# Between the layers of a graph attention kernel: rows started during the last matmuls, one wait per quotient, normalising in place

## The chip, the core and the metric

One core of a Trainium2 chip runs the whole program. The metric is device time in microseconds (us), smaller is better. Two kernels are compared by the median of several runs.

## The reference

x has 4096 rows (nodes) of 256 features; `adj` is a 4096 x 4096 matrix of zeros and ones. Four layers follow one another, each as `x = layernorm(x + gnn(x, adj))`:

```
# layer 0: h = x W (4 heads of 64); e = leaky_relu(s_src + s_dst, 0.01), masked by adj
#          out = elu(softmax(e) @ h)
# layer 1: the same with slope 0.2 and without elu
# layer 2: one head of 256 with slope 0.2, and four dense side branches and a gate
# layer 3: h = tanh(x W + b); softmax over one score per node, masked by adj; att @ (x W)
x = _layernorm(x + _L0_gnn_ref(x, adj, ...), axis=-1)
x = _layernorm(x + _L1_gnn_ref(x, adj, ...), axis=-1)
```

The change is at the two joints from layer 0 to 1 and from 1 to 2.

## The kernel before

The rows are held as T = 32 tiles of 128 rows; four tiles are a quad (QT = 4, QUADS = 8). `x` and `h` (a view of `hv`) stay in SBUF for all tiles. Each engine has its own program, written out in order by hand, and waits on counting semaphores; there is no scheduler.

**Attention of layers 0 and 1.** There are four passes, one for each head, of eight groups of 512 rows (`group` in the PE and DVE programs). DVE makes 0/1 masks from the packed adjacency, ACT marks which scores are above the bend, and PE multiplies the masks with the bf16 parts of the values, in banks 0 to 3 or 4 to 7 in turn. `evacuate` (DVE) adds up four banks into `sums`; `quotient` (POOL) divides and writes the group's rows of `h`. Group g's quotient of the last pass completes the rows of quad g, since a group and a quad are the same 512 rows. The last group's banks are summed by an `evacuate` at the end of `attention`, when PE has finished; POOL then makes the last quotient. `values` has two slots, one for even and one for odd passes; the last pass reads slot 1.

**Joint.** DVE's loop over layers does, for layers 1 and 2: `fold_weights(l)` (eight small operations on the new weights), a wait for the last quotient of all, and `between(l)`. For a quad, `norm_stats` adds h to x (layer 1: after an ELU), and makes mean and variance; POOL's `make_rstd` makes the inverse root; `normalize` writes the four normalised tiles to a staging tile `xs`, which is shared by all quads. In the loop of `between`, DVE normalises quad q-1 and then starts `norm_stats` of quad q. The ELU of a quad is max(h, exp(min(h, 0)) - 1): ACT's `elu_exp` makes `low` and then `ex`, and DVE combines. ACT waits with `elu_exp(q)` until DVE has used `ex` of quad q-1, for there is one tile of each.

**Product.** For each quad, PE's `dense` transposes the eight blocks of `xs` into banks 0 and 1; ACT copies them to `xT` in two pieces; PE multiplies with the weights into banks 2 to 5 (sixteen matmuls), and ACT copies h and the scores of each tile out. From layer 1 on, ACT also copies `xs` back into `x`, and DVE waits for that (`s_xkept`) before the next `normalize`. In layer 0, POOL's `stage_x` copies x to `xs`, and PE packs the adjacency (`pack`) between the quads. All these are loops over q with registers (`Fori`).

The order in ACT's layer 1 is `elu_exp(0)`, then for q = 1 to 7 `elu_exp(q)` and `dense(1, q-1)`, then `dense(1, 7)`.

After the last quad come the scores' maximum, the exponentials and the first values, and then the next attention.

## Time and profile before

| what | value |
|---|---|
| median of 3 runs | 3223.1 us (3221.91 to 3226.79) |
| the profiled execution, its own time | 3223.3 us |
| its span, first to last instruction | 3221.5 us |
| PE busy (matmuls) | 2984.2 us, 93% |
| DVE, ACT, POOL busy | 69%, 60%, 38% |
| mean granted clock of PE | 0.973 |
| opening stage with layer 0's product | 24 to 81 us |
| joint of layers 0 and 1, last matmul to last copy of h | about 906 to 987 us |
| joint of layers 1 and 2, the same | about 1716 to 1777 us |

The page lists for each engine how long it was busy; a timeline lists single instructions with their start, their duration and, in brackets, how long the engine stood idle before them and what released it. VectorE is DVE, ScalarE is ACT, GpSimd is POOL in such rows. The granted clock is the share of full speed that TensorE had.

### The profile page before, as it was taken

To read this page: it belongs to the slowest core of one execution; us is meant where nothing else is said; L and a number is where in the kernel's file an instruction comes from. 1 tells how busy PE (TensorE), PEld (TensorE's weight loads), DVE (VectorE), ACT (ScalarE), POOL (GpSimd) and SP (SyncE) were. 2 spreads that over 40 slices of the span, in tenths; PEclk is the share of its full clock that TensorE was granted. 3 is DMA by queue.
4 is the path that set the end of the run, shared out by engine and by line. 5 is a ranking of instruction groups with operands and counts; after the bars stand their busy time and mean duration, and the time that the engine had idled before them with its cause. 6 is when DMAs were issued, how large, how long until landed. Compare 5 with 4: busy or idle time off the path is not lost.

```text
span 3221.5 us, 73270 instructions
## 1 busy us (share of the span) xinstructions
PE 2984.2 (93%) x26664; PEld 2737.6 (85%) x26664; DVE 2219.1 (69%) x4102; ACT 1932.2 (60%) x3404; POOL 1213.0 (38%) x1646
## 2 busy tenths in 40 slices
PE   6588899999966999999997899999999999879997
PEld 5588899999955999999996778778878878669997
DVE  4888688887767888788776555666666656554447
ACT  4565799999957999989995444444444544420000
POOL 2333454751212646565222013333333233534433
PEclk9899999999988999999999999999999999989999
DMA  7576000000100000000010000000000000000001
GB/s 267 185 251 217 11 10 13 14 10 14 67 0 11 13 14 10 13 12 12 14 42 0 14 4 4 1 4 4 1 4 4 1 1 1 2 1 1 0 0 52
DMA packets 42292, 104.64 MB, mean 32 GB/s; under 512 B 9904, under 2 KB 23472, under 8 KB 33968
## 3 DMA queue, kind: packets, MB, share of 16 engines
q1 hardware_dynamic: 42160, 102.92, 9.6%
q8 instruction: 78, 1.28, 0.2%
q14 instruction: 54, 0.44, 0.0%
HBM read 98.51 MB, written 4.39 MB: 32 GB/s over the span
## 4 chain that ended last, share of the span: by engine, by line
PE 85%; DVE 5%; issue 3%; DMA 2%; ACT 2%; POOL 1%; SPq 0%; DVEq 0%; POOLq 0%; ACTq 0%
PE bank L1104 21%; PE bank L1101 21%; PE bank L1147 15%; PE bank L1185 12%; PE bank L1107 11%; DMA arena<-in_adj_dram 2%; PE bank L1174 2%; PE bank L1065 2%; PE bank L1161 1%; PE bank L1079 1%; DVE arena L1414 1%; DVE sums L1624 1%; PE bank L1291 0%; DVE rings L1691 0%; POOL lnst L545 0%
## 5 line engine op out<-in xcount | busy, mean ns | idle before, releaser
L1101 PE MATMUL bank<-values,rings 128*128 128x195 bf16 x8192 | 1415.4, 247 | 91.6 <-DVE sums L1624 46.7
L832 ACT ACTIVATE above<-srow,kpass 128x512 fp8e4<-128x512 f32 x2048 | 1288.8, 709 | 213.2 <-DVE rings L1694 202.7
L1104 PE MATMUL bank<-values,rings 128*128 128x195 bf16 x8192 | 1415.3, 249 | 0.0
L1101 PEld LDWEIGHTS bank<-values,rings 128*128 128x128 fp8e4 x8192 | 809.4, 99 | 102.0 <-issue 98.4
L1104 PEld LDWEIGHTS bank<-values,rings 128*128 128x128 fp8e4 x8192 | 787.2, 96 | 1.2
L1691 DVE TENSOR_TENSOR rings<-rings,above 128x512 uint32<-128x512 uint32 x512 | 390.2, 762 | 240.5 <-PE bank L1104 208.9
L850 ACT ACTIVATE values<-srow,cmul 128x512 f32<-128x512 f32 x256 | 206.0, 815 | 432.8 <-PE bank L1185 431.8
L1694 DVE TENSOR_TENSOR rings<-rings 128x512 uint32<-128x512 uint32 x512 | 427.8, 836 | 17.5
L1185 PE MATMUL bank<-hv,values 128*128 128x257 f32 x1792 | 423.1, 381 | 10.0 <-DVE values L1568 10.0
L1185 PEld LDWEIGHTS bank<-hv,values 128*128 128x128 f32 x1792 | 336.4, 191 | 80.7 <-issue 25.5
L1107 PE MATMUL bank<-values,rings 128*128 128x195 bf16 x4096 | 348.0, 248 | 19.0 <-DVE rings L1682 19.0
L1107 PEld LDWEIGHTS bank<-values,rings 128*128 128x128 fp8e4 x4096 | 347.5, 97 | 19.7 <-issue 19.4
L577 POOL TENSOR_TENSOR quot<-sums,cmul 128x260 f32<-128x260 f32 x64 | 45.6, 712 | 714.2 <-DVE sums L1624 714.2
L1685 DVE TENSOR_SCALAR rings<-packed 128x512 uint32 (+1 forms) x512 | 245.5, 479 | 2.1 <-issue 1.4
L1682 DVE TENSOR_SCALAR rings<-packed 128x512 uint32 (+1 forms) x256 | 116.4, 455 | 175.1 <-PE bank L1107 173.2
L1568 DVE SCALAR_TENSOR_TENSOR values<-values,cmul,rings 128x512 f32<-128x512 f32 x256 | 192.9, 761 | 43.9 <-ACT values L850 43.5
L661 POOL TENSOR_SCALAR zrow<-zrow 128x1 f32<-128x1 f32 x128 | 47.6, 372 | 446.1 <-DVE zrow L1765 446.1
L1624 DVE TENSOR_REDUCE sums<-bank 128x130 f32<-128x390 f32 (+1 forms) x396 | 181.7, 487 | 14.9 <-PE bank L1104 13.2
L1147 PE MATMUL bank<-arena,above 128*128 128x256 f32 (+1 forms) x496 | 165.9, 482 | 0.8 <-ACT above L905 0.8
L1147 PEld LDWEIGHTS bank<-arena,above 128*128 128x128 f32 x496 | 94.0, 190 | 53.1 <-issue 43.9
L507 POOL TENSOR_TENSOR values<-vtmp_pool,values 128x260 f32 (+1 forms) x120 | 109.4, 912 | 25.5 <-POOL values L504 21.2
L1147 PE MATMUL bank<-quot,arena 128*128 128x256 f32 x512 | 118.3, 379 | 0.0
(202 smaller groups left out, 3500.5 us busy)
## 6 DMA issues: line engine op xcount, KB each, us to landing
arena<-in_adj_dram SPq DMA_DIRECT2D x64, 1024.0 KB, 5.5
srow<-src_dram SPq DMA_DIRECT2D x72, 256.0 KB, 3.2
x<-in_x_dram SPq DMA_DIRECT2D x1, 4096.0 KB, 14.2
out_dram<-x SPq DMA_DIRECT2D x8, 512.0 KB, 2.9
arena<-in_L_gnn_fe_w_dram SPq DMA_DIRECT2D x2, 512.0 KB, 10.0
arena<-in_L_gnn_W_hz_dram SPq DMA_DIRECT2D x1, 1024.0 KB, 10.5
arena<-in_L_gnn_g_w_dram SPq DMA_DIRECT2D x1, 1024.0 KB, 11.4
weights<-in_L_gnn_W_dram SPq DMA_DIRECT2D x3, 256.0 KB, 3.4
```

The lines of the kernel that those rows point to most:

```text
L832: last = act.activation(above[:, k % 2, q, :], srow[:, par, :], ACT.Relu, scale=BIG, bias=kpass[:, slot, q * BITS + k:q * BITS + k + 1], s ...
L850: act.activation(w2[:, m % DEPTH, :], srow[:, g % 2, :], ACT.Relu, scale=b_col[:, jt:jt + 1], bias=c_neg[:, jt:jt + 1]).then_inc(E.relu, 1)
L1101: pe.matmul(acc[:, 0:KW], pos[:, k % 2, q, :].bitcast(FP8)[:, rows], v[:, 0:KW], start=first, stop=final, skip_group_check=True)
L1104: last = pe.matmul(acc[:, KW:2 * KW], neg[:, k % 2, q, :].bitcast(FP8)[:, rows], v[:, KW:2 * KW], start=False, stop=final, skip_group_chec ...
L1107: last = pe.matmul(acc[:, 0:KW], edge[:, k % 2, q, :].bitcast(FP8)[:, rows], v[:, 0:KW], start=first, stop=final)
L1147: last = pe.matmul(dst, lhsT[k], rhs[k], start=(k == 0), stop=(k == len(lhsT) - 1))
L1185: last = pe.matmul(bank[it][:, 0:VW], w2[:, m % DEPTH, it * P:(it + 1) * P], hv[:, q * BITS + k, :], start=(k == 0 and q == 0), stop=False)
L1568: dve.scalar_tensor_tensor(out=w2[:, m % DEPTH, :], in0=w2[:, m % DEPTH, :], scalar=c_pos[:, jt:jt + 1], in1=edge[:, unit % 2, q, :].bitca ...
L1624: return dve.tensor_reduce(sums[:, slot, it, 0:kinds, :], parts, AX.X, ALU.add)
L1685: dve.tensor_scalar(edge[:, r], words, shift[0], ONE, shift[1], ALU.bitwise_and)\
L1691: dve.tensor_tensor(pos[:, r], edge[:, r], above[:, r].bitcast(U32), ALU.bitwise_and)\
L1694: dve.tensor_tensor(neg[:, r], edge[:, r], pos[:, r], ALU.bitwise_xor).then_inc(s_sides, 1)
```

## The change

- DVE: `evacuate` of the last group moves from the end of `attention` into `between`, behind the first quad's addition and statistics; so `fold_weights` also comes ahead of it. `between` waits for each quad's own quotient in place of the last of all. Its order is now: add and statistics of quad q, then `normalize` of q-1.
- `normalize` writes into x itself; PE transposes from x. The tile `xs`, POOL's `stage_x`, ACT's copy back and the semaphore `s_xkept` are gone.
- The statistics `lnst` have two buffers. The scratch `prod` of `fold_weights` lies in `vtmp_pool` in place of `neg`.
- ELU: three tiles `ex` in slot 0 of `values`, each made in place (no `low`); ACT makes those of quads 0 to 2 first, each after its own quotient, and that of quad q+3 ahead of the copies of quad q.
- The loops over quads in DVE's, ACT's, PE's and POOL's programs at these places are written out.

```diff
-NORM_LINKS = {1: 2, 2: 2}
...
-        prod = neg[:, :].rearrange("p s q w -> p (s q w)").bitcast(F32)[:, 0:2 * F].rearrange("p (s f) -> p s f", s=2)
-        lnst = sb("lnst", [P, QT, 16])
+        prod = vtmp_pool[:, 0].rearrange("p n c -> p (n c)")[:, 0:2 * F].rearrange("p (s f) -> p s f", s=2)
+        lnst2 = sb("lnst", [P, 2, QT, 16])
+        lnst = lnst2[:, 0]
...
-        low, ex, xs, xT = (tiles_room[:, i * QT * F:(i + 1) * QT * F] for i in range(4))
-        low, ex, xs = (m.rearrange("p (t f) -> p t f", t=QT) for m in (low, ex, xs))
+        xT = tiles_room[:, 0:QT * F]
+        ex = [vroom[:, i * QT * F:(i + 1) * QT * F].rearrange("p (t f) -> p t f", t=QT) for i in range(3)]
...
             def rstd_of_quads(l):
-                with pool.Fori(0, QUADS) as q:
-                    chain.enter(q, 1)
-                    make_rstd(l, q)
-                chain.leave(QUADS)
-
-            def stage_x():
-
-                pool.wait_ge(s_x, 16)
-                with pool.Fori(0, QUADS) as q:
-
-                    pool.wait_ge(s_xtps, q * 2 + 1)
-                    pool.nop(nofuse=True)
-                    pool.tensor_copy(xs, x[:, ds(q * QT, QT), :]).then_inc(s_xmade, QT)
+                for q in range(QUADS):
+                    make_rstd(l, q, lnst2[:, q % 2])
+                chain.settle()
...
-                if l > 0:
-
-                    act.wait_ge(s_xmade, q * QT + (l * T + QT))
-                    act.activation(x[:, ds(q * QT, QT), :], xs, ACT.Copy).then_inc(s_xkept, 1)
...
             def elu_exp(q):
-                act.wait_ge(s_eluadd, q + 1)
-                act.activation(low, h[:, ds(q * QT, QT), :], ACT.Relu, scale=-1.0).then_inc(s_elulow, 1)
+
+                act.wait_ge(s_quot, H * NG - NG + CREDIT + q + 1)
+                if q >= 3:
+                    act.wait_ge(s_eluadd, q - 2)
+                act.activation(ex[q % 3], h[:, q * QT:(q + 1) * QT, :], ACT.Relu, scale=-1.0).then_inc(s_elulow, 1)
                 act.wait_ge(s_elulow, q + 1)
-                act.nop(nofuse=True)
-                act.activation(ex, low, ACT.Exp, scale=-1.0).then_inc(s_eluexp, 1)
+                act.activation(ex[q % 3], ex[q % 3], ACT.Exp, scale=-1.0).then_inc(s_eluexp, 1)
...
                 if l == 1:
-                    act.wait_ge(s_quot, H * NG + CREDIT)
-                    elu_exp(0)
-                    with act.Fori(1, QUADS) as q:
+                    for q in range(3):
                         elu_exp(q)
-                        dense(l, q - 1)
-                    dense(l, QUADS - 1)
-                elif l == 3:
-                    pass
-                else:
-                    with act.Fori(0, QUADS) as q:
-                        dense(l, q)
+                if l < 3:
+                    for q in range(QUADS):
+                        if l == 1 and q + 3 < QUADS:
+                            elu_exp(q + 3)
+                        copy_quad_xT(l, q)
+                        copy_quad_h(l, q)
...
-                        pe.wait_ge(s_xmade, q * QT + (l * T + i + 1))
+                        if l > 0:
+                            pe.wait_ge(s_xmade, q * QT + (NORMS[l] * T + i + 1))
                         for k in range(2):
                             last = pe.transpose(bank[half][:, (i % 2 * 2 + k) * P:(i % 2 * 2 + k + 1) * P],
-                                                xs[:, i, k * P:(k + 1) * P], ident[:, :])
+                                                x[:, q * QT + i, k * P:(k + 1) * P], ident[:, :])
...
-                    with pe.Fori(0, QUADS) as q:
+                    for q in range(QUADS):
                         dense(l, q)
...
+            def add_to_x(l, q):
+
+                xq, hq = (m[:, q * QT:(q + 1) * QT, :] for m in (x, h))
+                dve.wait_ge(s_quot, l * H * NG - NG + CREDIT + q + 1)
                 if l == 1:
 
                     dve.wait_ge(s_eluexp, q + 1)
...
             def normalize(l, q):
-                if l <= last_layer:
-
-                    dve.wait_ge(s_xtps, q * 2 + (l * 2 * QUADS + 1))
-                    if isinstance(q, int) and q == 0:
-                        if l > 1:
-                            dve.wait_ge(s_xkept, (l - 1) * QUADS)
-                    else:
-                        dve.wait_ge(s_xkept, q + (l - 1) * QUADS)
+
+                st = lnst2[:, q % 2]
                 dve.wait_ge(s_rstd, q + (NORMS[l] * QUADS + 1))
                 for i in range(QT):
-                    xt = x[:, ds(q * QT + i, 1), :]
-                    normed = xs[:, i:i + 1, :] if l <= last_layer else xt
-                    dve.tensor_scalar(normed, xt, lnst[:, i, 6:7], lnst[:, i, 9:10], ALU.subtract, ALU.mult)\
+                    xt = x[:, q * QT + i, :]
+                    dve.tensor_scalar(xt, xt, st[:, i, 6:7], st[:, i, 9:10], ALU.subtract, ALU.mult)\
                         .then_inc(s_xmade, 1)
 
             def between(l):
 
-                norm_stats(l, 0)
-                chain.settle()
-                with dve.Fori(1, QUADS) as q:
-                    chain.enter(q - 1, NORM_LINKS[l])
-                    normalize(l, q - 1)
-                    norm_stats(l, q)
-                chain.leave(QUADS - 1)
+                for q in range(QUADS):
+                    add_to_x(l, q)
+                    quad_stats(l, q)
+                    if q == 0:
+                        evacuate(l - 1, 1, 1, H * NG)
+                    else:
+                        normalize(l, q - 1)
                 normalize(l, QUADS - 1)
+                chain.settle()
...
-                evacuate(l, 1, 1, H * NG)
...
-                    dve.wait_ge(s_quot, l * H * NG + CREDIT)
                     between(l)
```

## Rows read from the trace of the kernel before

**Rows 1.** The page's part 1: busy us (share of span) x instructions, by engine.

```profile
PE 2984.2 (93%) x26664; PEld 2737.6 (85%) x26664; DVE 2219.1 (69%) x4102; ACT 1932.2 (60%) x3404; POOL 1213.0 (38%) x1646
```

**Rows 2.** The table of stretches: busy us of each engine, granted clock, DMA.

```profile
core 0: us, PE busy (x) PEld busy (x) DVE busy (x) ACT busy (x) POOL busy (x), PEclk, DMA share, GB/s
24.00:81.00 57.00, 55.10 (x449) 47.36 (x449) 26.74 (x32) 32.57 (x88) 10.91 (x7) 1.00 0.74 258
...
939.65:948.00 8.35, 7.48 (x28) 5.34 (x28) 6.09 (x17) 4.77 (x13) 1.27 (x2) 0.80 0.00 0
...
965.00:973.60 8.60, 4.67 (x22) 3.36 (x20) 5.01 (x14) 7.06 (x15) 1.27 (x2) 1.00 0.00 0
...
1746.70:1771.40 24.70, 20.93 (x97) 15.05 (x97) 17.20 (x53) 15.45 (x44) 5.08 (x8) 1.00 0.00 0
```

**Rows 3.** Timeline, layer 0 to 1: start, duration, engine, line, operation; brackets: idle before.

```profile
897.59 2.56 ACT L832 ACTIVATE above<-srow,kpass 128x512 fp8e4<-128x512 f32 x4 [1.04 <-DVE rings L1694]
...
901.38 0.69 DVE L1694 TENSOR_TENSOR rings<-rings 128x512 uint32<-128x512 uint32 x1
906.04 1.97 DVE L1624 TENSOR_REDUCE sums<-bank 128x130 f32<-128x390 f32 x4 [3.97 <-PE bank L1104]
...
911.61 0.06 DVE L1406 MEMSET credits<- 128x1 f32 x1
915.15 1.23 DVE L1435 SCALAR_TENSOR_TENSOR values<-values,hv 128x1024 f32<-128x1024 f32 x1 [3.49 <-ACT values L781]
...
919.32 0.38 DVE L1452 BATCH_NORM_AGGREGATE lnst<-lnst 128x2 f32<-128x6 f32 x4
921.84 1.38 DVE L1468 TENSOR_SCALAR values<-x,lnst 128x256 f32 x4 [2.14 <-POOL lnst L545]
...
908.26 0.62 POOL L577 TENSOR_TENSOR quot<-sums,cmul 128x260 f32<-128x260 f32 x1 [9.03 <-DVE sums L1624]
...
912.20 0.62 POOL L600 TENSOR_TENSOR hv<-quot 128x256 f32 x1 [0.24 <-POOL quot L586]
...
922.30 1.97 PE L1056 MATMUL bank<-ident,values 128*128 128x128 f32 x8 [16.30 <-DVE values L1468]
```

**Rows 4.** Timeline of the same joint: last copies of three quads, PE's transposes and products.

```profile
930.03 0.18 ACT L772 ACTIVATE scores<-bank 128x8 f32 x1
...
937.26 0.18 ACT L772 ACTIVATE scores<-bank 128x8 f32 x1
...
986.90 0.18 ACT L772 ACTIVATE scores<-bank 128x8 f32<-128x8 f32 x1
...
933.02 3.83 PE L1065 MATMUL bank<-weights,values 128*128 128x264 f32 x16 [1.52 <-ACT values L762]
...
939.65 1.41 PE L1056 MATMUL bank<-ident,values 128*128 128x128 f32 x8 [2.81 <-DVE values L1468]
941.10 5.51 PE L1065 MATMUL bank<-weights,values 128*128 128x264 f32 x16
```

**Rows 5.** Timeline, layer 1 to 2: VectorE's last mask, first transposes, last copies of quads.

```profile
1711.26 0.69 DVE L1694 TENSOR_TENSOR rings<-rings 128x512 uint32<-128x512 uint32 x1
1715.92 1.98 DVE L1624 TENSOR_REDUCE sums<-bank 128x130 f32<-128x390 f32 x4 [3.97 <-PE bank L1104]
...
1728.15 1.97 PE L1056 MATMUL bank<-ident,values 128*128 128x128 f32 x8 [12.27 <-DVE values L1468]
...
1735.83 0.19 ACT L772 ACTIVATE scores<-bank 128x8 f32 x1
...
1741.15 0.18 ACT L772 ACTIVATE scores<-bank 128x8 f32 x1
...
1777.09 0.18 ACT L772 ACTIVATE scores<-bank 128x8 f32 x1
```

**Rows 6.** Timeline of GpSimd: an operation of a quotient, and one after a gap.

```profile
873.38 1.17 POOL L578 TENSOR_TENSOR quot<-sums,cmul 128x260 f32<-128x260 f32 x1
...
108.61 1.42 POOL L494 TENSOR_TENSOR vtmp_pool<-hv,emul 128x256 f32<-128x256 f32 x1 [6.93 <-issue]
```

More of the change, by code:

```diff
@@ L478, in _ @@
             with sp.Fori(0, QUADS) as q:
[L479 removed]
+                sp.wait_ge(s_xmade, q * QT + (T * NORMS[4] + QT))
                 sp.dma_start(out[ds(q * (QT * P), QT * P), :].rearrange("(t p) f -> p t f", p=P),
@@ L537, in _, with make_rstd @@
             chain.settle()
-            def make_rstd(l, q):
+            def make_rstd(l, q, st=lnst):
                 pool.wait_ge(s_var, q + (NORMS[l] * QUADS + 1))
                 pool.nop(nofuse=True)
-                pool.tensor_scalar(lnst[:, :, 8:9], lnst[:, :, 7:8], EPS, None, ALU.add).then_inc(s_pool, 1)
+                pool.tensor_scalar(st[:, :, 8:9], st[:, :, 7:8], EPS, None, ALU.add).then_inc(s_pool, 1)
                 pool.wait_ge(s_pool, chain.next())
-                pool.tensor_tensor(lnst[:, :, 9:10], lnst[:, :, 8:9],
+                pool.tensor_tensor(st[:, :, 9:10], st[:, :, 8:9],
                                    minus_half.unsqueeze(2).to_broadcast([P, QT, 1]), ALU.pow)\
@@ L742, in _ @@
                     dense2()
-                if l == 0:
-                    stage_x()
-                elif l < 3:
+                if 0 < l < 3:
                     rstd_of_quads(l)
@@ L757, in _, with copy_quad_xT @@
         def _(act):
-            def dense(l, q):
+            def copy_quad_xT(l, q):
                 for half in range(2):
@@ L1043, in _ @@
             if last_layer == 0:
-                act.wait_ge(s_quot, H * NG + CREDIT)
-                with act.Fori(0, QUADS) as q:
+                for q in range(QUADS):
                     elu_exp(q)
@@ L1426, in pack @@
                 store_packed(t)
-            def norm_stats(l, q):
-                xq, hq = (m[:, ds(q * QT, QT), :] for m in (x, h))
+            def add_to_x(l, q):
+                xq, hq = (m[:, q * QT:(q + 1) * QT, :] for m in (x, h))
+                dve.wait_ge(s_quot, l * H * NG - NG + CREDIT + q + 1)
                 if l == 1:
                     dve.wait_ge(s_eluexp, q + 1)
-                    dve.nop(nofuse=True)
-                    dve.scalar_tensor_tensor(out=ex, in0=ex, scalar=-1.0, in1=hq, op0=ALU.add, op1=ALU.max)\
-                        .then_inc(s_dve, 1)
+                    dve.scalar_tensor_tensor(out=ex[q % 3], in0=ex[q % 3], scalar=-1.0, in1=hq, op0=ALU.add,
+                                             op1=ALU.max).then_inc(s_dve, 1)
@@ L1437, in norm_stats @@
                     dve.wait_ge(s_dve, chain.next())
-                    dve.nop(nofuse=True)
-                    dve.tensor_tensor(xq, xq, ex, ALU.add).then_inc(s_eluadd, 1)
-                    dve.wait_ge(s_eluadd, q + 2)
-                    dve.nop(nofuse=True)
-                elif l in (2, 4):
+                    dve.tensor_tensor(xq, xq, ex[q % 3], ALU.add).then_inc(s_eluadd, 1)
+                    dve.wait_ge(s_eluadd, q + 1)
+                else:
                     dve.tensor_tensor(xq, xq, hq, ALU.add).then_inc(s_dve, 1)
@@ L1444, in norm_stats, with quad_stats @@
                     dve.wait_ge(s_dve, chain.next())
-                    dve.nop(nofuse=True)
+            def quad_stats(l, q):
+                st = lnst2[:, q % 2]
                 for i in range(QT):
-                    last = dve.bn_stats(lnst[:, i, 0:6], x[:, ds(q * QT + i, 1), :].squeeze(1))
+                    last = dve.bn_stats(st[:, i, 0:6], x[:, q * QT + i, :])
                 last.then_inc(s_dve, 1)
                 dve.wait_ge(s_dve, chain.next())
-                dve.nop(nofuse=True)
@@ L1451, in norm_stats @@
                 for i in range(QT):
-                    last = dve.bn_aggr(lnst[:, i, 6:8], lnst[:, i, 0:6])
+                    last = dve.bn_aggr(st[:, i, 6:8], st[:, i, 0:6])
                 last.then_inc(s_var, 1)
             def normalize(l, q):
-                if l <= last_layer:
-                    dve.wait_ge(s_xtps, q * 2 + (l * 2 * QUADS + 1))
-                    if isinstance(q, int) and q == 0:
-                        if l > 1:
-                            dve.wait_ge(s_xkept, (l - 1) * QUADS)
-                    else:
-                        dve.wait_ge(s_xkept, q + (l - 1) * QUADS)
+                st = lnst2[:, q % 2]
@@ L1471, in between @@
             def between(l):
-                norm_stats(l, 0)
-                chain.settle()
-                with dve.Fori(1, QUADS) as q:
-                    chain.enter(q - 1, NORM_LINKS[l])
-                    normalize(l, q - 1)
-                    norm_stats(l, q)
-                chain.leave(QUADS - 1)
-                normalize(l, QUADS - 1)
+                for q in range(QUADS):
+                    add_to_x(l, q)
+                    quad_stats(l, q)
+                    if q == 0:
+                        evacuate(l - 1, 1, 1, H * NG)
+                    else:
+                        normalize(l, q - 1)
@@ L1482, in first_values @@
+                normalize(l, QUADS - 1)
+                chain.settle()
             def first_values(l):
```

12 lines of the change are left out of this document (3 added, 9 removed).

## The prediction

> **What bounds the kernel now.** I read the page's busy shares first. PE is busy for 93% of the span [rows 1], so an edit outside PE's work can pay only where PE stands still. The table of stretches then shows what each stage is. In the opening loop PE is busy 55.10 of 57.00 us, so at most 1.9 us can be won there. In the two stretches between layers it is not full: 7.48 of 8.35 us at a granted clock of 0.80, and 4.67 of 8.60 us at 1.00 [rows 2]. Last I read the timeline across the two joints, where the change lies.
>
> From layer 0 to 1 the reader should follow a chain [rows 3]: PE ends its pass just before 906.04; VectorE sums the last banks (1.97 us); GpSimd makes the last quotient (908.26 to 912.82); ScalarE does the first ELU; VectorE adds and takes statistics (915.15 to 919.70); GpSimd's inverse root follows and VectorE normalises at 921.84; PE transposes at 922.30. Every step waits for the one before. Yet VectorE had been idle since 902.07, and ScalarE since 900.15. After that, each group of four row tiles (a quad) costs 8.1 us on average: the last copy of h ends at 930.21 for quad 0 and at 987.08 for quad 7, 56.9 us for seven [rows 4]. From layer 1 to 2, without ELU, transposes start at 1728.15 and those ends are 1736.02 and 1777.27: 41.25 us for seven, 5.9 each [rows 5].
>
> **The change part by part.** The two joints are counted to the end of the last copy of h; what follows (scores, shifts, first values) is untouched.
>
> Start of joint 0 to 1. `fold_weights(1)` no longer stands behind `evacuate`, and its scratch has moved out of `neg`, so it can run while PE multiplies. Its eight operations take 908.01 to 911.67, say 3.7 us [rows 3], now from 902.2 to 905.9. Then `add_to_x(1, 0)` and `quad_stats(1, 0)`: 4.55 us, from the row at 915.15 to the end of the row at 919.32, to 910.5. ELU of quads 0, 1 and 2 starts on ScalarE at 900.2, with two passes of about 1.1 us each, and is never late. Only now comes `evacuate`, 4.5 us later than before; it ends at 912.5, and the last quotient can begin at 912.8. That quotient took 4.56 us. Behind it on GpSimd is the inverse root of quad 0, though its statistics are long done; GpSimd to normalise takes about 1.75 us (the 2.14 us wait of the row at 921.84 less the 0.4 us hand-over that has passed), and the first transposes stand 0.46 us behind. Without any disturbance they start at 919.6.
>
> There is one: `add_to_x(1, 1)` with its 1.22 us operations now runs beside the quotient. In the middle of a pass, beside VectorE's work, one of the quotient's operations took 1.17 us [rows 6], and one of the same shape 0.62 [rows 3]. Bounds: nothing, or two whole adds (2.4 us). I take 1.2, halfway, since the operations that lengthened it there were shorter. So transposes start at 920.8, against 922.30: 1.5 us won, though 4 us of VectorE's work was taken forward.
>
> This is where a page bears on it. The Trainium skill (SBUF — State Buffer, "Who interferes with whom") says that a VectorE instruction with two SBUF inputs and a GpSimd one that reads SBUF exclude each other for the whole instruction. By that rule both adds could stand in the quotient's way, and this start would win 0.3 us, not 1.5. The 1.17 us row agrees in direction; no row here has the long add beside a quotient.
>
> Steady part of joint 0 to 1. Quad 0 takes as long as before from transposes to last copy (922.30 to 930.21, 7.91 us), since PE is as cold: 928.7. The next four quads still have an ELU ahead of their copies on ScalarE, now that of quads 4 to 7. A quad whose transposes are almost ready is in the trace: from the last copy of quad 0, 930.21, to that of quad 1, 937.44, with the ELU in between, 7.23 us [rows 4]. The removed 1.05 us copy of xs to x lay beside PE's first products there, so it saves nothing on that path. What the change removes is the wait of the other quads for VectorE: ELU, add, statistics, root and normalise were one chain (the idle 2.81 us of the row at 939.65). VectorE now needs 4.55 + 1.3 = 5.9 us per quad without a wait, because quad q+1's add fills the wait for quad q's root. That is under 7.23, so ScalarE sets the pace. Four quads: 28.9 us, to 957.6. Quads 5, 6 and 7 have no ELU; such a quad is in joint 1 to 2: from 1736.02 to 1741.33, 5.3 us, with VectorE's wait still partly in it; I take 5.2. That gives 973.2 against 987.08, 13.9 us won with PE at full clock.
>
> The clock. At 933.02 PE's sixteen products took 3.83 us; at 941.10, after it had stood idle 2.81 us, 5.51, with the granted clock at 0.80 over that stretch, so part of it at the lower of its levels (1.2 instead of 2.4 GHz) [rows 2, 4]. Such a quad costs 1.7 us more. In the changed kernel PE does its transposes directly behind the products and then stands for 7.23 - 3.83 - 1.04 = 2.4 us (ELU and copy). That lies between the idle piece that came before the drop (2.81) and the one of quad 1 (1.52) that did not. I take two of the four ELU quads as cooled: 3.3 us given back. Bounds: none, and all four (6.7).
>
> Joint 1 to 2. VectorE is free at 1711.95 [rows 5]. Folding 3.7, add 1.3, statistics 1.9, so `evacuate` begins at 1719.1 instead of 1715.92 and ends at 1721.1; quotient 4.56 plus 0.6 for one add beside it; root, normalise: transposes at 1728.7. That is 0.55 us later than now: the early start does not pay here, because the last quotient is the longer leg. Then 7.87 us for quad 0 as before and 7 x 5.2, PE's and ScalarE's own pace, where it was 41.25: the end is 1773.0 against 1777.27, 4.3 us won. VectorE needs about 4.5 us per quad here, and the stretch 1746.70 to 1771.40 has it busy 17.20 of 24.70 us, so it is not the limit.
>
> Layer 0. GpSimd's staging copies go and PE reads x directly; the copies ran beside PE's packing products. The whole stage can win 1.9 us at most [rows 2]; I take zero, because products and packing products follow one another on PE.
>
> Loops written out. Register work goes (0.2 us between ELU's two operations on VectorE, not on the new path); more instructions have to be fetched. One stall in the trace, 6.93 us on GpSimd at 108.61 in front of an instruction with no releaser, may be of that kind [rows 6]; I take zero, that row is the upper price of one.
>
> Sum: 13.9 - 3.3 + 4.3 = 14.9 us. The profiled execution took 3223.3 us (span 3221.5) and the median is 3223.1, so they are the same to 0.2 us. Forecast: 3223.1 - 14.9 = 3208.2, say 3208. Best case: no cooling (+3.3), no disturbance (+1.8), layer 0 (+1.9): 3201. Worst of the same mechanism: all four cooled (-3.4), two full adds at the first joint and one at the second (-1.8): 3213.4.
>
> **The rivals.**
> A. PE stays at full clock throughout: 18.2 us won, 3205. For: quad 1 kept full clock. Against: the new idle time is in one piece.
> B. All four ELU quads cool, and the quotient is held by whole adds: 3213.4, the worst case above. For: the 5.51 us rows. Against: 2.4 is less than 2.81 us.
> C. The early start backfires: whatever VectorE does ahead of `evacuate` is added to the quotient's chain. That costs a gain only if quad 0 (folding, add, statistics) starts late; it now ends 4.5 and 3.2 us after PE, and each further us is a us of the total. If folding, say, still stood behind PE's end (waiting for something), evacuation would be 3.8 us later at both joints, and the total 3208.2 + 7.6 = 3215.8.
> D. Slower: the written-out code is fetched late where an engine enters it for the first time. At 6.93 us each the gain of 14.9 us is gone from 2.2 stalls on, and three exposed ones (20.8 us) give 3208.2 + 20.8 = 3229. Against: that row stands alone in the trace, though code written out is entered in each layer. The Trainium skill (Runtime: NRT & Kernel Launch, "Instruction fetch mechanics") holds that straight code is prefetched and that taken branches are what stalls, which would speak for no stall at all; no run here shows it.
> E. The change does nothing measurable: only if VectorE, not ScalarE and PE, still set the pace; a time of 3220. Against: its 5.9 us per quad.
>
> **How the numbers follow.** The forecast case (3206.5 to 3210.5) has 0.42; A (3201 to 3206.5) 0.25; B 0.15; C 0.10; D 0.04; E 0.04. Range 3200 to 3216: it takes in A, B and nearly all of C, and leaves out D and E. A change of 0.2% (6.4 us, so under 3216.7) is about what can be told from none. Faster 0.91: forecast, A, B, C with 0.01 off for its tail; same 0.05: E and that tail; slower 0.04: D.
>
> **What the profile after would show.** Transposes of joint 0 to 1 at about 15 us after PE's last product; ELU rows on ScalarE before it; last copies of h 7.2 us apart for four quads, then 5.2; joint 1 to 2 at 5.2 throughout, with its first transposes no earlier than now. Wrong if h copies wait for VectorE's normalise, if idle time without releaser stands at the entry of a stage, or if the first transposes come later than 17 us after PE's end.

## The result, and the profile after

The changed kernel took 3209.45 us (median of 8 runs, 3202.32 to 3217.78), the kernel before 3225.9 us beside it (8 runs, 3221.91 to 3227.71). The ratio is 0.9954, 95% interval 0.9939 to 0.9968: faster by 0.46%. Forecast were 3208 us and, against 3223.1, a ratio of 0.9953. That the two agree so closely is partly luck: several terms were off, in both directions. The profiled execution is the fastest of its eight, 3202.32 us, so what the other executions lose more is not in its trace.

The page after, part 1, which answers to [rows 1]:

```profile
PE 2971.1 (93%) x26664; PEld 2735.4 (85%) x26664; DVE 2218.5 (69%) x4101; ACT 1907.5 (60%) x3381; POOL 1202.6 (38%) x1638
```

ScalarE lost the copy of the normalised rows, GpSimd the staging of x; PE's matmuls are the same in number. The timeline of the kernel after at the joint from layer 0 to 1, which answers to [rows 3]; VectorE first, then GpSimd, then PE:

```profile
902.78 0.69 DVE L1670 TENSOR_TENSOR rings<-rings 128x512 uint32<-128x512 uint32 x1
903.51 0.42 DVE L1375 TENSOR_TENSOR vtmp_pool<-weights,avec 128x256 f32<-128x256 f32 x1
...
907.25 1.23 DVE L1417 SCALAR_TENSOR_TENSOR values<-values,hv 128x1024 f32<-128x1024 f32 x1
...
911.21 0.38 DVE L1434 BATCH_NORM_AGGREGATE lnst<-lnst 128x2 f32<-128x6 f32 x4
911.50 1.94 DVE L1600 TENSOR_REDUCE sums<-bank 128x130 f32<-128x390 f32 x4
913.36 1.22 DVE L1417 SCALAR_TENSOR_TENSOR values<-values,hv 128x1024 f32<-128x1024 f32 x1
914.61 1.53 DVE L1420 TENSOR_TENSOR x<-x,values 128x1024 f32<-128x1024 f32 x1
...
921.05 1.38 DVE L1443 TENSOR_SCALAR x<-x,lnst 128x256 f32<-128x256 f32 x4 [3.05 <-POOL lnst L544]
...
913.70 1.36 POOL L566 TENSOR_TENSOR quot<-sums,cmul 128x260 f32<-128x260 f32 x1 [13.05 <-DVE sums L1600]
915.02 1.60 POOL L567 TENSOR_TENSOR quot<-sums,cmul 128x260 f32<-128x260 f32 x1
...
918.91 0.62 POOL L589 TENSOR_TENSOR hv<-quot 128x256 f32 x1 [0.24 <-POOL quot L575]
919.63 0.26 POOL L542 TENSOR_SCALAR lnst<-lnst 128x4 f32<-128x4 f32 x1
...
921.61 1.94 PE L1038 MATMUL bank<-ident,x 128*128 128x128 f32 x8 [14.20 <-DVE x L1443]
923.47 5.80 PE L1047 MATMUL bank<-weights,values 128*128 128x264 f32 x16
...
932.42 3.80 PE L1047 MATMUL bank<-weights,values 128*128 128x264 f32 x16 [2.28 <-ACT values L749]
...
939.37 3.80 PE L1047 MATMUL bank<-weights,values 128*128 128x264 f32 x16 [2.28 <-ACT values L749]
```

Folding and the first quad's addition now stand before the sums of the last banks. Then the reader should stop at 911.59, when the first quad's statistics are done: its inverse root is made only at 919.63, because on GpSimd it stands behind the last quotient (913.70 to 919.53). VectorE waits 3.05 us for it, and PE 14.20. VectorE's own order holds quad 0 back too: ahead of normalising it stand the sums and the second quad's addition and statistics (913.36 to 918.00).

Timeline of ScalarE in the kernel after, the last copies of quads 0, 1, 5 and 7 (they answer to [rows 4]):

```profile
929.58 0.18 ACT L757 ACTIVATE scores<-bank 128x8 f32<-128x8 f32 x1
...
936.53 0.18 ACT L757 ACTIVATE scores<-bank 128x8 f32<-128x8 f32 x1
...
962.39 0.18 ACT L757 ACTIVATE scores<-bank 128x8 f32<-128x8 f32 x1
...
972.42 0.18 ACT L757 ACTIVATE scores<-bank 128x8 f32<-128x8 f32 x1
```

The first four steps are 6.95 us each, the last three 5.01 (972.42 - 962.39 = 10.03 for two). The table of stretches after (columns as in [rows 2]), over the ELU quads, over the others and over joint 1 to 2:

```profile
929.60:957.40 27.80, 18.69 (x98) 15.59 (x97) 24.67 (x67) 19.21 (x50) 5.28 (x9) 1.00 0.00 1
957.40:972.40 15.00, 13.68 (x69) 11.04 (x67) 2.33 (x7) 8.65 (x31) 1.11 (x2) 1.00 0.01 1
1721.60:1756.70 35.10, 32.39 (x166) 26.65 (x163) 19.61 (x64) 20.29 (x72) 6.37 (x10) 1.00 0.00 1
```

The granted clock is 1.00 in all three. In the first, PE is still busy only 18.69 of 27.80 us; in the others 13.68 of 15.00 and 32.39 of 35.10. Joint 1 to 2 after, VectorE, GpSimd and PE (answers to [rows 5]):

```profile
1697.50 0.69 DVE L1670 TENSOR_TENSOR rings<-rings 128x512 uint32<-128x512 uint32 x1
...
1706.94 1.36 POOL L566 TENSOR_TENSOR quot<-sums,cmul 128x260 f32<-128x260 f32 x1 [11.59 <-DVE sums L1600]
...
1711.77 0.26 POOL L542 TENSOR_SCALAR lnst<-lnst 128x4 f32<-128x4 f32 x1
...
1713.75 1.94 PE L1038 MATMUL bank<-ident,x 128*128 128x128 f32 x8 [11.63 <-DVE x L1443]
```

To say where the time went I cut both profiled executions at the same rows: at VectorE's last mask of an attention and at the last copy of scores of a joint.

| stretch, us | before | after | difference |
|---|---|---|---|
| to the last mask of layer 0 | 901.38 | 902.78 | +1.40 |
| joint 0 to 1 (to the last copy) | 85.52 | 69.64 | -15.88 |
| attention of layer 1 | 724.36 | 725.08 | +0.72 |
| joint 1 to 2 | 65.83 | 59.20 | -6.63 |
| all behind it | 1444.41 | 1443.80 | -0.61 |
| span | 3221.5 | 3200.5 | -21.0 |

The joints give 22.5 us, more than the 14.9 of the forecast; the medians differ by only 16.5. The table itself, which is of the fastest execution, shows only 1.5 of the missing 6 us. So the experiments have two questions: what sets the joints now, and where 6 us of their gain go.

### The profile page after: what moved, and what is told of

The parts are those of the page before. It is cut to its first block, busy times and chain, and to the rows that moved or that the text cites. A ratio compares the mean times of both kernels' runs of the same rounds, so it can differ in the third digit from the quotient of the medians.

```text
span 3200.5 us, 72283 instructions
## 1 busy us (share of the span) xinstructions
PE 2971.1 (93%) x26664; PEld 2735.4 (85%) x26664; DVE 2218.5 (69%) x4101; ACT 1907.5 (60%) x3381; POOL 1202.6 (38%) x1638
## 3 DMA queue, kind: packets, MB, share of 16 engines
q8 instruction: 83, 1.36, 0.2%
## 4 chain that ended last, share of the span: by engine, by line
PE 84%; issue 5%; DVE 4%; DMA 3%; ACT 2%; POOL 1%; DVEq 0%; POOLq 0%; SPq 0%; ACTq 0%
PE bank L1086 21%; PE bank L1083 20%; PE bank L1129 15%; PE bank L1167 12%; PE bank L1089 11%; DMA arena<-in_adj_dram 2%; PE bank L1156 2%; PE bank L1047 2%; PE bank L1143 1%; DVE arena L1396 1%; DVE sums L1600 1%; DVE rings L1667 0%; PE bank L1273 0%; PE bank L1061 0%; ACT rings L882 0%
## 6 DMA issues: line engine op xcount, KB each, us to landing
x<-in_x_dram SPq DMA_DIRECT2D x1, 4096.0 KB, 14.3
arena<-in_L_gnn_fe_w_dram SPq DMA_DIRECT2D x2, 512.0 KB, 10.3
```

## The experiments

Each edit is to the changed kernel unless it says otherwise. "Joints" are the two stretches of the table above.

**The changed kernel again.** No edit.

> The changed kernel once more, for a second profile and more times. Its eight times so far lie between 3202.3 and 3217.8 us, where those of the kernel before lie within 5.8 us, and the profiled one is the fastest. Theory P: the spread is TensorE's clock in the four ELU quads of joint 0 to 1; none of them was cooled in that profile, and in slower executions one to four are, 1.7 us each, so at most 6.7 us. Theory Q: the spread lies elsewhere (the opening stage and the first attention, where the adjacency is loaded), and the joint lasts 69.6 us from VectorE's last mask to the last copy of scores in any profile.

3207.22 us (5 runs, 3204.47 to 3208.94), 0.9946 (0.9933 to 0.9960). Last mask of layer 0 at 906.35, joints 70.34 and 59.35. One quad's products took 5.49 us in place of 3.80; the granted clock was 0.69 from 935.0 to 940.5, so part of them stood at the lower clock level (1.2 instead of 2.4 GHz). Both theories hold in part: one quad was cooled, but the joint is only 0.7 us longer, while the last mask comes 3.6 us later. Its PE timeline:

```profile
927.03 4.81 PE L1047 MATMUL bank<-weights,values 128*128 128x264 f32 x16
...
935.00 5.49 PE L1047 MATMUL bank<-weights,values 128*128 128x264 f32 x16 [2.28 <-ACT values L749]
...
943.63 3.80 PE L1047 MATMUL bank<-weights,values 128*128 128x264 f32 x16 [2.28 <-ACT values L749]
```

Idle pieces of 2.28 us stand in front of the slow quad and of the fast one behind it, so such a piece alone does not cool PE.

**The early start undone.**

```diff
                 for q in range(QUADS):
                     add_to_x(l, q)
                     quad_stats(l, q)
-                    if q == 0:
-                        evacuate(l - 1, 1, 1, H * NG)
-                    else:
+                    if q > 0:
                         normalize(l, q - 1)
...
+                evacuate(l, 1, 1, H * NG)      # at the end of attention(l)
```

> Only the early start is undone: the last banks are summed at the end of attention, ahead of fold_weights and of quad 0's addition; one wait per quotient, ELU three ahead and x in place stay. Theory: the early start is worth the little that the last quotient's path shows, because the inverse root of quad 0 stands behind that quotient on GpSimd. In the changed kernel transposes start 14.2 us after the end of PE's last product at the first joint and 11.5 at the second. With the banks summed first: sums 2.0, quotient 4.6 beside folding, and VectorE's folding 3.7, addition 2.5, statistics 1.9, root 1.8, 0.5: 12.5 us at the first joint and 11.2 at the second, so 2 us faster than the changed kernel in all (3207 to 3208). Rival: work taken forward is gained whole, then this one is 8.3 plus 6.9 us slower than the changed kernel.

3206.91 us (5 runs, 3204.78 to 3209.32), 0.9947 (0.9934 to 0.9961). From the last mask to the first transposes it took 19.6 and 16.7 us, where the changed kernel takes 18.8 and 16.3. So putting VectorE's work ahead of the last sums is worth 0.8 and 0.4 us in that kernel, nothing that the whole shows. The rival (8.3 and 6.9 us) is out, but the forecast was wrong in direction: this start should have been the earlier one. Timeline of this kernel, VectorE, GpSimd, PE:

```profile
919.05 0.38 DVE L1434 BATCH_NORM_AGGREGATE lnst<-lnst 128x2 f32<-128x6 f32 x4
919.35 1.19 DVE L1417 SCALAR_TENSOR_TENSOR values<-values,hv 128x1024 f32<-128x1024 f32 x1
...
923.57 0.70 DVE L1443 TENSOR_SCALAR x<-x,lnst 128x256 f32<-128x256 f32 x2
...
920.73 1.97 POOL L544 TENSOR_TENSOR lnst<-lnst,exponents 128x4 f32<-128x4 f32 x1
...
924.10 1.94 PE L1038 MATMUL bank<-ident,x 128*128 128x128 f32 x8 [14.96 <-DVE x L1443]
```

The last quotient took 5.1 us and ended at 916.50, before quad 0's statistics (919.43), so it no longer holds the root up. What ends last is VectorE's own order, which the forecast left out: quad 1's addition and statistics (919.35 to 923.66) stand ahead of normalising quad 0.

**The inverse root of quad 0 ahead of the last quotient.** VectorE's order changes too: it normalises quad 0 directly behind the last sums, ahead of quad 1's addition.

```diff
             def rstd_of_quads(l):
-                for q in range(QUADS):
+                for q in range(1, QUADS):
...
-                        with pool.Fori(0, NG // 2) as gg:
+                        with pool.Fori(0, NG // 2 - 1) as gg:
...
-                        chain.leave(NG)
+                        chain.leave(NG - 2)
+                        quotient(l, p, NG - 2, 0)
+                        make_rstd(l + 1, 0, lnst2[:, 0])
+                        quotient(l, p, NG - 1, 1)
+                        chain.settle()
...
                     if q == 0:
                         evacuate(l - 1, 1, 1, H * NG)
-                    else:
+                        normalize(l, 0)
+                    elif q > 1:
                         normalize(l, q - 1)
```

> The changed kernel, with the inverse root of quad 0 ahead of the last quotient on GpSimd, and VectorE normalises quad 0 directly behind the sums of the last banks. If the quotient in front of the root is what eats the early start, transposes start as soon as the last banks are summed: at the first joint about 7.6 us earlier (913.4 instead of 921.05 for the first normalising), at the second 6.3 us (1706.9 instead of 1713.2), together 13.9 us less than the changed kernel, about 3195.5. Rival: PE then waits for VectorE or for the last quotient later in the joint, and half or less arrives: 3202 or more.

3195.64 us (4 runs, 3191.65 to 3200.95), 0.9907 (0.9892 to 0.9922); joints 66.58 and 53.71. Timeline of this kernel, VectorE, GpSimd, PE:

```profile
919.19 1.94 DVE L1605 TENSOR_REDUCE sums<-bank 128x130 f32<-128x390 f32 x4
921.17 2.55 DVE L1447 TENSOR_SCALAR x<-x,lnst 128x256 f32<-128x256 f32 x4
...
920.09 1.04 POOL L544 TENSOR_TENSOR lnst<-lnst,exponents 128x4 f32<-128x4 f32 x1
...
923.71 2.02 POOL L575 TENSOR_TENSOR quot<-quot,exponents 128x4 f32<-128x4 f32 x1
...
921.73 1.86 PE L1042 MATMUL bank<-ident,x 128*128 128x128 f32 x6 [6.62 <-DVE x L1447]
...
932.55 1.72 PE L1042 MATMUL bank<-ident,x 128*128 128x128 f32 x8 [3.48 <-DVE x L1447]
```

PE waits 6.62 us instead of 14.20. The first transposes come 11.25 us after the last mask (910.48), 7.6 earlier than in the changed kernel, as forecast. Two moves share this. By the rows of the kernel after, the wait for the root behind the quotient was 3.05 us, and quad 1's addition and statistics ahead of the normalising took 4.64 (913.36 to 918.00); the sum, 7.69, is about what was won. In joint 1 to 2 the same two pieces are 3.51 and 3.07 us, together the 6.58 that were won there. Neither move was made alone, and the root first with VectorE's late start was not run, so what the early start is worth there is not shown. Part goes back at quad 1. PE waits 3.48 us for it, because VectorE now normalises quad 1 only behind quad 2's addition and statistics. And joint 0 to 1 had two quads partly at the lower clock level (5.08 and 5.49 us).

**ELU between the two kinds of copies.** The ELU of quad q+3 behind the copies to xT instead of ahead of them.

```diff
+                        copy_quad_xT(l, q)
                         if l == 1 and q + 3 < QUADS:
                             elu_exp(q + 3)
-                        copy_quad_xT(l, q)
                         copy_quad_h(l, q)
```

> The changed kernel, with the ELU of quad q+3 on ScalarE behind the copies of the transposes of quad q instead of ahead of them, so that it lies beside PE's products. If ScalarE's order sets the pace of the four ELU quads (6.95 us in the profile after, 5.01 for the three without), each of them falls to 5.0 to 5.5: 6 to 8 us less than the changed kernel, 3201.5 to 3203.5. Then VectorE's 5.5 us per quad may set it. Rival: PE's products wait for the copies of h out of their banks, which now stand behind the ELU, and nothing is won.

3197.54 us (5 runs, 3194.08 to 3200.91), 0.9920 (0.9906 to 0.9933), 4 us under the forecast; joints 62.49 and 58.08. Joint 0 to 1 gained 7.15 us, within the forecast 6 to 8. Joint 1 to 2 has no ELU; 1.1 us of its 59.20 went because its first products took 4.56 us here and 5.67 in after. One quad of this kernel, VectorE then PE:

```profile
943.45 1.35 DVE L1443 TENSOR_SCALAR x<-x,lnst 128x256 f32<-128x256 f32 x4
...
948.96 1.35 DVE L1443 TENSOR_SCALAR x<-x,lnst 128x256 f32<-128x256 f32 x4
...
943.89 1.41 PE L1038 MATMUL bank<-ident,x 128*128 128x128 f32 x8 [0.18 <-DVE x L1443]
945.43 3.80 PE L1047 MATMUL bank<-weights,values 128*128 128x264 f32 x16
```

The pace is 5.0 to 5.1 us for three steps and then 5.5 for three, VectorE's own (948.96 - 943.45), with no idle time between its rows; PE waits 0.18 us a quad. The ELU's 2.1 us lay in PE's way only by its place in ScalarE's order.

**Layer 0's part undone.** GpSimd stages x to a tile again, and PE's and ScalarE's loops over quads of layer 0 are loops with registers again; layers 1 and 2 stay written out.

```diff
+            def stage_x():
...
+                    pool.wait_ge(s_xtps, q * 2 + 1)
+                    pool.nop(nofuse=True)
+                    pool.tensor_copy(xs, x[:, ds(q * QT, QT), :]).then_inc(s_xkept, QT)
...
+                if l == 0:
+                    with act.Fori(0, QUADS) as q:
+                        copy_quad_xT(l, q)
+                        copy_quad_h(l, q)
...
-                    for q in range(QUADS):
-                        dense(l, q)
-                        if l == 0:
+                    if l == 0:
+                        with pe.Fori(0, QUADS) as q:
+                            dense(l, q)
                             pack(q)
+                    else:
+                        for q in range(QUADS):
+                            dense(l, q)
```

> The changed kernel with layer 0's part of the change undone: POOL's staging copies, and TensorE's and ScalarE's loops over the quads of layer 0 with registers, as before; the joints keep the change. The four profiles of changed kernels so far reach VectorE's last mask of layer 0 at 902.8 to 906.4 us (910.5 in the one with the root first), before 901.4, and differ by then, while the joints repeat within 1 us. Theory F: the written-out code of the opening stage has to be fetched while the adjacency is loaded, and that costs the 1 to 5 us and the spread; then this kernel is at 3202 to 3205 with a spread of at most 5 us. Rival G: it is the adjacency's transfers, which vary whatever the code; then 3206 to 3209 and the same spread as the changed kernel.

3202.98 us (6 runs, 3200.16 to 3217.41), 0.9938 (0.9920 to 0.9955). Five of the six are at 3206.9 or below, where the changed kernel's runs lie at 3202 to 3218, but the intervals overlap. Last mask at 905.45, joints 70.36 and 59.49. The median fits theory F, the one run at 3217.41 and the late mask fit G, and staging came back together with the loops. That alone settles nothing.

**Both improvements.** The root first and the ELU inside, run twice.

> Root of quad 0 ahead of the last quotient, and ELU of quad q+3 behind the copies of the transposes, together. Alone they gave 11.6 and 9.7 us less than the changed kernel. They touch different stretches (start of both joints, pace of the first), so they add up: 3186 to 3188. If quad 1, whose root now stands behind the last quotient, comes late for a PE that starts 7 us earlier, 2 to 4 us of it are lost: 3188 to 3191.

> The changed kernel with the inverse root ahead of the last quotient and the ELU between the two copies, a second time. Its joints should repeat: 60.3 and 53.7 us, within 1 us or 1.7 us where a quad's products are cooled. With the spread of the opening its median should lie at 3189 to 3196 us, the ratio at 0.989 to 0.992.

First 3192.72 us (5 runs, 3192.37 to 3200.62), 0.9906 (0.9892 to 0.9919), then 3190.3 us (4 runs, 3189.61 to 3193.16), 0.9901 (0.9884 to 0.9917). Joints 60.33 and 53.69, and 60.30 and 53.69: 9.3 and 5.5 us below the changed kernel. The first time missed both forecasts (3186 to 3188 and 3188 to 3191), the second lies in the lower gain's. The two gains of joint 0 to 1, 3.1 and 7.1 us by themselves, do not add up in full: PE still waits 3.48 us for quad 1. This is the fastest version here, 1% under the kernel before.

**ELU one quad ahead only.**

```diff
-                    for q in range(3):
-                        elu_exp(q)
+                    elu_exp(0)
...
-                        if l == 1 and q + 3 < QUADS:
-                            elu_exp(q + 3)
+                        if l == 1 and q + 1 < QUADS:
+                            elu_exp(q + 1)
```

> The changed kernel with ELU one quad ahead instead of three. VectorE normalises quad q only behind the addition of quad q+1, which needs that quad's ELU, which ScalarE now makes only behind the copies of quad q-1. Theory: the depth of ELU and VectorE's order hang together, and the chain ELU 2.1, addition 2.5, statistics 1.8, normalise 0.45, transposes 0.65, copy 0.6, products and copies of h 4.4 us is paid in full by six quads: 12.5 us each, 37 us slower than the changed kernel, about 3245, slower than before. Rival: VectorE is far enough ahead and the depth matters little: within 5 us of the changed kernel.

3248.83 us (4 runs, 3246.68 to 3250.11), 1.0071 (1.0056 to 1.0086): slower than before by 0.7%, though all else of the change is there. The forecast was 3245. Steps are 13.7 to 13.9 us. The chain of one quad in this kernel, ScalarE, VectorE, PE:

```profile
948.78 1.06 ACT L766 ACTIVATE values<-values 128x1024 f32<-128x1024 f32 x1
...
949.93 1.23 DVE L1416 SCALAR_TENSOR_TENSOR values<-values,hv 128x1024 f32<-128x1024 f32 x1 [8.27 <-ACT values L766]
...
954.63 1.97 PE L1037 MATMUL bank<-ident,x 128*128 128x128 f32 x8 [7.31 <-DVE x L1442]
956.52 4.56 PE L1046 MATMUL bank<-weights,values 128*128 128x264 f32 x16
```

VectorE normalises quad q-1 only behind the statistics of quad q, which need the ELU of q. That ELU stands on ScalarE behind the copies of quad q-2. So the steps of one quad follow those of another in a ring. The distance of the ELU is what opens it.

**The copy of the normalised rows put back.**

```diff
             def copy_quad_h(l, q):
+                if l > 0:
+                    act.wait_ge(s_xkept, (l - 1) * QUADS + q)
+                    act.activation(tiles_room[:, QT * F:2 * QT * F].rearrange("p (t f) -> p t f", t=QT),
+                                   x[:, q * QT:(q + 1) * QT, :], ACT.Copy).then_inc(s_xkept, 1)
```

> The changed kernel with ScalarE's 1.05 us copy of a normalised quad put back behind the copies of the transposes in both joints (16 times, into a tile that nobody reads). Theory: it lies beside PE's first products, where ScalarE stands idle 0.82 us before the first copy of h and 0.43 before each further one, so it costs nothing: within 2 us of the changed kernel. Rival: ScalarE is what sets the pace, so all of it counts, 16.8 us.

3205.05 us (6 runs, 3204.28 to 3209.87), 0.9941 (0.9929 to 0.9953); joints 69.72 and 59.30. The 1.05 us copy costs nothing that the joints or the whole show: it lies beside PE's first products.

**The kernel before, again.** In every changed kernel the last mask of layer 0 comes later than in before (902.8 to 910.5 over ten profiles). Is that the change?

> The kernel before, profiled once more, to see where its own time varies. In the profiles of the changed kernels VectorE's last mask of layer 0 lies anywhere from 902.8 to 910.5 us, and in the one profile of before at 901.38. Theory (the opening's transfers vary whatever the code): before too will show it later this time, 903 to 908, with joints of 85.5 and 65.8 us as before, and a ratio of 1.000. Rival (the change itself made the opening later and less steady): before repeats 901.4 within 0.5 us.

3223.34 against 3223.18 us, 1.0001 (0.9991 to 1.0010). Its last mask is at 900.42, its joints 84.59 and 65.81. So the later mask comes with the change. In after it arises in layer 0's first pass, in which the adjacency is still loaded and converted. The timeline of VectorE in this profile of before, the first and the seventh sum of banks:

```profile
104.69 1.97 DVE L1624 TENSOR_REDUCE sums<-bank 128x130 f32<-128x390 f32 x4
320.28 1.97 DVE L1624 TENSOR_REDUCE sums<-bank 128x130 f32<-128x390 f32 x4
```

The same two in the profile after (some of a sum's four rows are missing from this trace):

```profile
105.89 1.03 DVE L1600 TENSOR_REDUCE sums<-bank 128x130 f32<-128x390 f32 x2
323.88 1.50 DVE L1600 TENSOR_REDUCE sums<-bank 128x130 f32<-128x390 f32 x3
```

That is 215.6 us against 218.0; the first profile of before has 216.2. By the view of waits, VectorE waited 9.5 us for the adjacency's transfers in that stretch here (10.3 in the first profile of before), and 11.9 us in after. In the other changed kernels the stretch took 218.6 to 222.1 us, with up to 15.2 us of such waits, though the code of that pass is the same.

**Two suspects, each added alone to the kernel before.** The place of tiles in SBUF:

```diff
-        lnst = sb("lnst", [P, QT, 16])
+        lnst2 = sb("lnst", [P, 2, QT, 16])
+        lnst = lnst2[:, 0]
```

> The kernel before, with lnst allocated for two quads as in the changed kernel, the second never used: all that lies behind it in SBUF (exponents, credits, the identity, powers) moves by 256 bytes. From the first to the seventh sum of layer 0's first pass, where the adjacency is loaded and converted, the two profiles of before took 216.2 and 215.6 us, and those of ten changed kernels 218.0 to 222.1. If the place in SBUF does it, this one takes 218 us or more, and 3225.5 us or more in all. If not, 215 to 216.5 us, and 3223.

3225.11 us (10 runs) against 3224.45, 1.0002 (0.9992 to 1.0011): no cost that the whole shows. Its first pass took 217.3 us, between the two forecasts, so the place may have a small part in that stretch; this is open. And the written-out loops:

```diff
-                    with act.Fori(1, QUADS) as q:
+                    for q in range(1, QUADS):
                         elu_exp(q)
                         dense(l, q - 1)
...
-                    with act.Fori(0, QUADS) as q:
+                    for q in range(QUADS):
                         dense(l, q)
...
-                    with pe.Fori(0, QUADS) as q:
+                    for q in range(QUADS):
                         dense(l, q)
```

> The kernel before, with the quads' loops of PE and ACT written out, as in the changed kernel, nothing else. If more code (fetched while the adjacency is loaded, or stored elsewhere) is what makes layer 0's first pass longer, the stretch from its first to its seventh sum takes 218 us or more in place of 216, and the whole 3225.5 us or more. If neither this nor the place in SBUF does it: 215 to 216.5 us, and 3222 to 3224 (at most 0.1 us per quad of register work goes).

3231.99 us (10 runs, 3222.81 to 3236.49) against 3224.45 (19 runs, 3220.93 to 3228.70): 1.0026 (1.0017 to 1.0036). **Writing the loops out cost 7.5 us by itself here**, and spread the runs over 14 us. The profiled run is again the fastest of its ten, 9.2 us under its median, so it shows only a small part: first pass 218.3 us, last mask at 903.29. Where the other executions lose the rest is in no trace. In the joint the written-out loops even win (83.90 against 84.4 to 85.5 in three profiles of looped kernels). The queues that bring instructions, over the first 325 us of this kernel (packets, MB, share of the engines):

```profile
q8 instruction: 7, 0.11, 0.1%
q14 instruction: 6, 0.05, 0.0%
```

The same two of the changed kernel with layer 0 looped again:

```profile
q8 instruction: 3, 0.05, 0.1%
q14 instruction: 5, 0.04, 0.0%
```

Before has 4 and 5 there, after 7 and 6. So layer 0's written-out code brings 4 or 5 more packets of instructions into the stretch in which the adjacency uses the DMA engines. But the kernel with layer 0 looped has as few as before, and its first pass still took 219.4 us. So that the loops cost this in the kernel before is shown once, over ten runs; by what way is open, and these fetches alone do not explain it.

One reading over all runs points to layer 0. Take from the gain of the joints (against the first profile of before) the gain of the whole in the medians. What is lost elsewhere is then 6.1 us in after and 2.2 to 4.9 us in the eight other profiles with all loops written out. With layer 0 looped it is -0.7 us, nothing lost. The interval of that kernel is wide (its gain is 14.5 to 25.8 us), so this is a sign and no proof.

## Why the prediction was right, and where it was not

**What bounds the kernel** was right: in the two profiles the joints moved by 22.5 us, all else together by 1.5, and PE stays at 93%.

**Start of joint 0 to 1.** Forecast 1.5 us won; last mask to transposes went from 20.92 to 18.83, 2.1 won. The quotient was lengthened by 1.27 us (4.56 to 5.83) where 1.2 was taken: its two first operations took 1.36 and 1.60 us beside the adds, 0.62 and 0.90 before. The forecast took the 4.56 us as undisturbed, but it lay beside the folding: the same second operation took 0.62 us in joint 1 to 2 after. The page "SBUF — State Buffer" of the Trainium skill ("Who interferes with whom") has such pairs exclude each other; the trace agrees in that both rows of the quotient are longer, but both adds together cost 1.27 us, not 2.4. The root behind the quotient was named as the last wait, rightly, and it was (3.05 us). That quad 1's addition and statistics stand right behind it in size, 4.64 us in VectorE's order, was not seen; the root-first kernel won both. The forecast did not part the early start from the rest either. The late-start experiment gives it 0.8 us; the other 1.3 come with one wait per quotient and the ELUs made ahead.

**Pace.** The mechanism was right, the forecast time per quad too long: ScalarE's chain sets 6.95 us (forecast 7.23), other quads 5.01 (5.2), seven quads 42.8 instead of 44.5. VectorE needs 5.51, forecast 5.9. Most of the difference to 7.23 is the loops' register work, which was held to lie off this path: written out and with nothing else changed, the same step of before took 7.01 us.

**The clock.** This step failed: 3.3 us was given back where none was in the profile after. Two of four ELU quads were to be cooled by a 2.4 us idle piece. The piece is there (2.28 us), but with it no quad was cooled in the profile after and none with the copy put back, and one (1.7 us) in the repeat, the late start and with layer 0 looped, each time the second quad. With the root first it was the second and third, the third behind such a piece. So in these kernels a drop was seen only in the first three quads after the long standstill, and from one execution of the same kernel to another it comes or not: 5.80 + 3.80 us for the first two quads after, 4.81 + 5.49 in the repeat. Before, the 2.81 us stood ahead of the transposes, after, the 2.28 stand behind them; whether that matters is open. More idle time does not mean a higher price, though: with ELU one ahead PE waited 7.31 us ahead of the transposes, and sixteen products took 4.45 to 4.67 us. Rival A (full clock throughout) describes the profile after.

**Joint 1 to 2.** Forecast 4.3 us won, measured 6.63. The start was forecast 0.55 later and came 0.64 earlier (16.89 to 16.25): the one add cost the quotient 0.3 us in place of 0.6 (4.86 against 4.56), and `evacuate` could begin 7.25 us after the last mask (1704.75 - 1697.50), not 7.8. Of this difference 0.25 us is a slip in adding: 1711.95 + 3.7 + 1.3 + 1.9 is 1718.85, not 1719.1. Seven quads took 35.1 us instead of 36.4.

**Layer 0 and the loops.** Taken as zero, and this is the term that failed most: written-out loops cost 7.5 us alone in the kernel before, and 2.2 to 6.1 us are missing outside the joints in the changed kernels that have them. Rival D had the place wrong (stalls where an engine enters the code, 6.93 us each) and had 0.04 of the chance; a gap like that of the 6.93 us row stands at the same place in seven profiles compared, looped or not (6.92 to 7.29 us), so it was no sign of it. The page "Runtime: NRT & Kernel Launch" of the Trainium skill ("Instruction fetch mechanics") has straight code prefetched in order, and taken branches that leave the loaded part stall; by it written-out loops are free or better. The joint agrees (83.90 us), the whole does not (+7.5 us), and the measurement decides. By what way the longer program loses time no run shows.

**The sum.** 14.9 us were made of 10.6 for joint 0 to 1 (measured 15.9; in the repeat against the second profile of before, 84.59 - 70.34 = 14.3), 4.3 for joint 1 to 2 (6.6), and nothing elsewhere. Elsewhere about 6 us were lost at the median (16.5 - 22.5), which the written-out loops' 7.5 us would cover; that they are the same loss was argued, not measured. So two errors nearly cancelled: joints forecast 7.6 us too small, and a loss of 6 us taken as nothing. The close number is luck; the joints as the place, the last wait and the pace were foreseen.

## What to carry to other kernels

When an engine has finished a tile's last input, look at what stands ahead of the tile on the next engine's queue, and on its own. Moving a 1.3 us root past a quotient that nobody needed yet, and the normalising past the next quad's addition, won 8.6 us in two joints. Taking 4 us of work forward without that had won 1.2. A step that another engine waits for goes ahead of one that fills time (the ELU behind the xT copies: 7.1 us in one joint). Unroll a loop only where its register work is on the path, and time it by itself over some ten runs: here one profile, and of the fastest run at that, hid most of its cost.

## What was not expected of the hardware

- Normalising four tiles took 2.55 us beside the first operations of the last quotient, and 1.38 us in after, where only the small operations of a root ran beside it (rows 921.17 of the root-first kernel and 921.05 of after). The quotient's small power, 1.02 us in after, took 2.02 in the root-first kernel, beside VectorE's next additions. So either engine can lose.
- Instruction packets are few (7 and 6 in 325 us), yet the longer program cost the kernel before 7.5 us and widened the spread of its runs from 8 to 14 us. The spread alone proves nothing: the other written-out kernels had 3 to 9 us, the one with layer 0 looped 17.
- PE's first sixteen products after the standstill of joint 0 to 1 took 4.4 to 5.9 us with the same instructions. Between two executions of the changed kernel they took 5.80 and 4.81 us, and the second quad's 3.80 and 5.49.
